# Sandwich layer on one core: three tiles turned by DMA out of SBUF in place of TensorE, Hadamard product a unit later, new order

## Chip, core and metric

The kernel runs on one core of a Trainium2 chip, in one launch. The metric is the device time in microseconds, as the median of the runs. The profile is one execution, with times from the span's start.

## The reference

The input is x of 8 batches x 1024 tokens x 512 features, in float32. Cut to what matters:

```python
def attn(x):                          # 16 heads of 32, causal, score decay of -distance
    Q, K, V = heads(x @ Wq.T + bq), heads(x @ Wk.T + bk), heads(x @ Wv.T + bv)
    s = Q @ K.T / sqrt(32); s = where(future, -inf, s - distance)
    return merge(softmax(s) @ V) @ Wo.T + bo
def ffn(x):                           # H: 512 x 512 Hadamard matrix / sqrt(512)
    xh = x @ H
    scale = max(|xh|, row) / 7; xq = clip(round(xh / scale), -8, 7) * scale
    return xq @ ternary(weight).T
x = x + layernorm(attn(layernorm(x)))
x = x + layernorm(ffn(layernorm(x)))
```

## The kernel before

The 8192 tokens are cut into 32 units of 256 (two tiles t of 128), four units to a batch (PER = 4). A software pipeline runs over steps s. In step s the kernel works on unit n = s+1 (q, k, v products, norms, scores), unit s (keys, exponentials, weighting: the attention proper), unit k = s-1 (output product, first residual, the folded token) and unit k-1 (quantized levels, ternary product, output), while unit m = s+2 is loaded and normalised. Each engine runs its own hand-written list of calls in program order, and semaphores tie the lists together. The order of those lists sets everything, since an engine that waits holds up all that stands behind it. The SP queue is such a list too: it issues all loads and SBUF copies.

Products that must be near float32 are made from float16 pairs (high part, low part) as three matmuls: `split_product`, whose matmuls are all line 1030. `qk(n, g)` for g = 0 to 3 makes a group of q and of k, `values(n, t)` v, `out_product(k, t)` the attention output. The matmul needs the token tile with features on partitions, so the tile has to be turned:

- the normalised token tile: `front_tile` (L1059) turns the float32 tile `xin` on TensorE into a PSUM bank; ACT (`front_high`, L475) and DVE (`front_low`, L743) take the high and low part out of it into `xT`. `qk` and `values` read `xT`.
- the folded token tile (sum and difference of the two halves of x1, `fold`, L832/833): `turn_x2` (L1178), `x2_high` (L534), `x2_low` (L845); `transform` (L1188) then multiplies by the 256 x 256 Hadamard block.
- the level tile q (bfloat16): `find_scale` (DVE) and `round_levels`, `level` (ACT, L540, L546) make it from the Hadamard product; `turn_q` (L1196), `keep_q` (L551); `second` (L1206) multiplies by the ternary weights, and `scale_out`, `z_stats`, `z_columns`, `norm_z`, `finish_out` end the unit.

`keys(s, g, half)` (L1134) makes transposed scores for `exps` (L510, L514), POOL's `clear_future` (L386) clears the future, `weigh(s, g)` (L1154, L1159) multiplies by v. `scores(n, i)` (L1102 to L1114) makes the row maxima for `maxima` (DVE, L767) and needs the stacked q and k parts. Those are made by `restack(n)` on SP (L318): 12 DMAs from `stage` to `stacks`, issued when the last `qk_low_part(n, 3)` (DVE, L753) is done. `max_rows` (L334), `mix_values` (L326 to L328) and the loads of `xres` (L344) and `xin` (L279) are the rest of SP's list.

All products but keys and weighting share four PSUM banks. `ORDER` lists the 24 uses of a step; use i takes bank i % 4, and `claim` makes TensorE wait until the use before it in that bank is emptied.

Of the kernel before, what the change touches and what calls it, by code (L numbers as in the profile page):

```python
# [5 lines left out]
P = 128  # L6
# [27 lines left out]
TP = 2  # L34
# [4 lines left out]
ORDER = (("qk", 0), ("q", 0), ("max", 0), ("qk", 1), ("q", 1), ("qk", 2), ("f", 0), ("qk", 3),  # L39
         ("x", 0), ("f", 1), ("x", 1), ("y", 0), ("y", 1), ("v", 0), ("s", 0), ("norms", 0),  # L40
         ("s", 1), ("v", 1), ("turn", 0), ("turn", 1), ("s", 2), ("s", 3), ("h", 0), ("h", 1))
AHEAD = {"x": 2, "qk": 1, "v": 1, "norms": 1, "s": 1, "max": 0, "y": -1, "turn": -1, "h": -1, "q": -2, "f": -2}

# [22 lines left out]
def fast_path(nc, x, wqT, wkT, wvT, woT, bq, bk, bv, bo, wff, had16, identity, window, ident16,  # L66
# [3 lines left out]
    with ExitStack() as ctx:  # L70
# [20 lines left out]
        xT = [(sb(f"xTh{i}", [P, KC, W2], F16), sb(f"xTl{i}", [P, KC, W2], F16)) for i in range(2)]  # L91
# [9 lines left out]
        ident = sb("ident", [P, P], F32)  # L101
# [9 lines left out]
        xres = sb("xres", [P, TP, D], F32)  # L111
# [3 lines left out]
        x2T = (sb("x2Th", [P, KC, W2], F16), sb("x2Tl", [P, KC, W2], F16))  # L115

        q16 = sb("q16", [P, TP, D], BF16)
        qT = x2T[1][:].bitcast(BF16)
# [17 lines left out]
        y_veps, y_rstd, y_off = col(12), col(14), col(16)  # L136
# [33 lines left out]
        front_turned = sem("front_turned")  # L170
        xTh_made = sem("xTh_made")
        xTl_made = sem("xTl_made")
# [33 lines left out]
        xres_in = sem("xres_in")  # L206
# [8 lines left out]
        x2_turned = sem("x2_turned")  # L215
# [6 lines left out]
        q_turned = sem("q_turned")  # L222
        qT_made = sem("qT_made")
# [51 lines left out]
        def _(sp):  # L275
            def load_front(m):

                until(sp, front_turned, TP * (m - 1))
                sp.dma_start(xin[m % 2][:], rows_of(x, m)).then_inc(xin_in[m % 2], 16)  # L279
# [11 lines left out]
            load_front(0)  # L291
            sp.dma_start(ident[:], identity).then_inc(ident_in, 16)
            load_weights(0, wqT)
            load_weights(1, wkT)
            load_bias(bias[:, 0, :], bq)
            load_bias(bias[:, 1, :], bk)
            load_weights(2, wvT)
            load_weights(3, woT)
            load_bias(bias[:, 2, :], bv)
            load_bias(guard[:, 12:16], bo)  # L300
            sp.dma_start(ffstage, wff.rearrange("(c p) n -> p c n", p=P)).then_inc(ff_in, 16)
            load_front(1)
            sp.dma_start(sel[:], headsel).then_inc(consts_in, 16)
            sp.dma_start(window_sb[:], window).then_inc(consts_in, 16)
            sp.dma_start(identh[:], ident16).then_inc(consts_in, 16)
            sp.dma_start(had[:], had16.rearrange("(c p) n -> p c n", p=P)).then_inc(consts_in, 16)
            sp.wait_ge(w_low, 2)
            load_rows(0)
# [29 lines left out]
            for s in range(-1, STEPS + 1):  # L338
                if has(s):
                    max_rows(s)  # L340
                if has(s - 1):

                    until(sp, x1_made, TP * (s - 1))
                    sp.dma_start(xres[:], rows_of(x, s - 1)).then_inc(xres_in, 16)  # L344
                if has(s + 3) and s + 3 >= 2:
                    load_front(s + 3)
                if has(s + 1):
                    restack(s + 1)
                    mix_values(s + 1)
                if s == -1:  # L350
                    sp.wait_ge(w_low, 4)
                    sp.wait_ge(bv_product, 1)
                    load_rows(1)
                    sp.wait_ge(ff_step, FF_STEPS)
                    load_rows(2)

        @block.gpsimd
        def _(pool):
# [54 lines left out]
            for s in range(-1, STEPS + 2):  # L413
                n, m, k = s + 1, s + 2, s - 1
                if has(m):
                    front_root(m)
                if has(k):
                    heads_low(k, 3)
                if has(n):
                    square_of(n, 0)  # L420
                    square_of(n, 1)
# [3 lines left out]
                if has(k - 1):  # L425
                    z_root(k - 1)
                if has(k):
                    y_root(k)
                if has(s):
                    clear_future(s, 2)  # L430
                    heads_low(s, 0)
                    clear_future(s, 3)
                if has(k - 1):
                    finish_out(k - 1)
                if has(s):
                    heads_low(s, 1)
                    heads_low(s, 2)
# [7 lines left out]
        def _(act):  # L445
# [27 lines left out]
            def front_high(m, t):  # L473
                act.wait_ge(front_turned, TP * m + t + 1)
                nc.scalar.activation(xT[m % 2][0][:, :, t * P:(t + 1) * P],  # L475
                                     bank("x", t)[:].rearrange("p (c n) -> p c n", c=KC), ACT.Copy,
                                     scale=SX).then_inc(xTh_made, 1)
# [53 lines left out]
            def x2_high(k, t):  # L531
                act.wait_ge(x2_turned, TP * k + t + 1)
                until(act, h_product, TP * k + t - 1)
                nc.scalar.activation(x2T[0][:, :, t * P:(t + 1) * P],  # L534
                                     bank("turn", t)[:].rearrange("p (c n) -> p c n", c=KC), ACT.Copy,
                                     scale=SX).then_inc(x2h_made, 1)

            def round_levels(k, t):
                act.wait_ge(qinv_made, TP * k + t + 1)
                nc.scalar.activation(y[:, t, :], bank("h", t)[:], ACT.Identity, bias=round_col[:],  # L540
                                     scale=qinv[:, t:t + 1]).then_inc(rounded, 1)

            def level(k, t):
                act.wait_ge(rounded, TP * k + t + 1)
                until(act, q_turned, TP * (k - 1) + t + 1)
                nc.scalar.activation(q16[:, t, :], y[:, t, :], ACT.Identity, bias=unround_col[:]).then_inc(q_made, 1)  # L546

            def keep_q(k, t):
                act.wait_ge(q_turned, TP * k + t + 1)
                until(act, f_product, TP * k + t - 1)  # L550
                nc.scalar.activation(qT[:, :, t * P:(t + 1) * P],  # L551
                                     bank("q", t)[:, 0:D // 2].bitcast(BF16).rearrange("p (c n) -> p c n", c=KC),
                                     ACT.Copy).then_inc(qT_made, 1)
# [8 lines left out]
            nc.scalar.activation(identb[:], ident[:], ACT.Copy).then_inc(identb_made, 1)  # L562
            front_norm(0, 0)
            front_norm(0, 1)
            weights_high(0)
            front_high(0, 0)
            front_high(0, 1)
            weights_high(1)
            for s in range(-1, STEPS + 2):
# [5 lines left out]
                if has(k - 1):  # L575
                    level(k - 1, 1)
                if s == -1:
                    weights_high(2)
                if has(k - 1):
                    keep_q(k - 1, 0)  # L580
                if has(n):
                    qk_high_part(n, 1)
                if has(m):
                    front_norm(m, 0)
                if has(n):
                    qk_high_part(n, 2)
                if has(m):
                    front_norm(m, 1)
                if has(k - 1):
                    keep_q(k - 1, 1)  # L590
# [1290 lines left out]
```

## Time and profile before

| | us |
|---|---|
| median of 3 runs | 1300.65 (1299.8 to 1302.07) |
| time of the profiled execution | 1295.19 |
| its span | 1293.5 |
| PE busy (matmul) | 1198.1, 93% |
| DVE busy | 1008.5, 78% |
| ACT busy | 714.9, 55% |
| POOL busy | 569.2, 44% |
| SP's DMA queue, share of the 16 DMA engines | 33.3% |

The profiled execution lies 5.46 us below the median of the runs. The page's other parts are the span in slices, the chain of work that ended last (PE 71%, DVE 20%), the groups of instructions and the DMA issues. A busy share is a mean over start, steady part and end; the steady part is read from stretches of the trace.

### The profile page before, as it was taken

Reading aid. Unit: us, or ns where it says so; the run is one execution under the profiler, and the core shown is the slowest. Engines: PE = TensorE matmul, PEld = TensorE weight load, DVE = VectorE, ACT = ScalarE, POOL = GpSimd, SP = SyncE. Lnnn points to the kernel's source line nnn. Section 1 sums busy time; section 2 is a strip of 40 time slices with the busy share of each in tenths; the row PEclk is TensorE's granted clock in tenths of the full one; section 3 lists DMA queues with packets and bytes.
Section 4 is the critical chain, followed back from the end, with each engine's and each line's share of the span. In section 5 each row is a group of like instructions: output and inputs, shape, how many; then the busy total and the mean of one; then the engine's idle time right before and its main releaser. Section 6 shows DMA issues by size and latency. Waiting matters only on the chain.

```text
span 1293.5 us, 45441 instructions
## 1 busy us (share of the span) xinstructions
PE 1198.1 (93%) x19075; PEld 820.7 (63%) x19136; DVE 1008.5 (78%) x2456; ACT 714.9 (55%) x1523; POOL 569.2 (44%) x715
## 2 busy tenths in 40 slices
PE   2779999999999999999999999999999999999852
PEld 2456766666666766666667666667767666676431
DVE  3656887888887888888887888788887888877772
ACT  3444656555665665556556655565565565655531
POOL 0133354454544544544445445544553454444441
PEclk9889999999999999999999999999999999999875
DMA  7333333434344334343443343434433434344110
GB/s 249 90 76 100 101 100 85 115 84 115 85 117 116 89 95 116 84 114 86 116 116 90 95 117 84 115 85 116 116 89 95 116 85 115 84 100 99 53 49 18
DMA packets 69520, 128.50 MB, mean 99 GB/s; under 512 B 14880, under 2 KB 15392, under 8 KB 69216
## 3 DMA queue, kind: packets, MB, share of 16 engines
q1 hardware_dynamic: 64624, 108.50, 33.3%
q0 software_dynamic: 4688, 17.04, 3.5%
q8 instruction: 153, 2.51, 0.8%
q14 instruction: 55, 0.45, 0.1%
HBM read 41.09 MB, written 16.78 MB: 45 GB/s over the span
## 4 chain that ended last, share of the span: by engine, by line
PE 71%; DVE 20%; issue 3%; ACT 3%; SPq 1%; DMA 1%; POOL 0%; POOLq 0%; ACTq 0%; DVEq 0%
PE f_job L1030 41%; PE f_job L1188 5%; PE f_o L1154 5%; PE f_o L1159 4%; PE f_job L1206 4%; PE f_st L1134 3%; DVE f_bst L799 3%; PE f_job L1114 2%; DVE f_y L833 2%; PE f_job L1178 2%; DVE f_x L825 2%; PE f_job L1102 2%; DVE f_y L810 2%; DVE f_xTl L743 1%; PE f_job L1059 1%
## 5 line engine op out<-in xcount | busy, mean ns | idle before, releaser
L386 POOL TENSOR_SCALAR_AFFINE_SELECT f_PT<-f_PT 64x512 f32<-64x512 f32 (+1 forms) x256 | 180.6, 730 | 130.4 <-ACT f_PT L510 93.2
L753 DVE SCALAR_TENSOR_TENSOR f_stage<-f_job,f_bias,f_stage 128x256 f16<-128x256 f32 x256 | 112.0, 479 | 148.3 <-ACT f_stage L488 148.2
L392 POOL TENSOR_TENSOR f_OTl<-f_o,f_OTh 128x256 f16<-128x256 f32 x128 | 89.0, 695 | 290.7 <-ACT f_OTh L528 290.1
L521 ACT ACTIVATE f_inverse<-f_o 128x256 f32<-128x256 f32 x128 | 49.1, 383 | 244.1 <-PE f_o L1159 244.1
L488 ACT ACTIVATE f_stage<-f_job,f_bias 128x256 f16<-128x256 f32 x256 | 106.6, 467 | 109.9 <-PE f_job L1030 109.9
L1030 PE MATMUL f_job<-f_xTh,f_wqh 128*128 128x256 f16 x512 | 140.4, 274 | 7.1 <-DVE f_wkl L652 6.8
L1030 PE MATMUL f_job<-f_xTl,f_wqh 128*128 128x256 f16 x512 | 140.1, 274 | 0.0
L1030 PE MATMUL f_job<-f_xTh,f_wkh 128*128 128x256 f16 x512 | 140.1, 274 | 0.0
L1030 PE MATMUL f_job<-f_xTh,f_wql 128*128 128x256 f16 x512 | 140.1, 274 | 0.0
L1030 PE MATMUL f_job<-f_xTh,f_wkl 128*128 128x256 f16 x512 | 140.1, 274 | 0.0
L1030 PE MATMUL f_job<-f_xTl,f_wkh 128*128 128x256 f16 x512 | 140.0, 273 | 0.0
L401 POOL TENSOR_TENSOR f_square<-f_stage 128x512 bf16<-128x512 f16 x128 | 129.4, 1041 | 15.0 <-ACT f_stage L488 14.9
L510 ACT ACTIVATE f_PT<-f_st 128x512 f32<-128x512 f32 x192 | 108.2, 592 | 30.3 <-PE f_st L1134 30.2
L1030 PE MATMUL f_job<-f_wvh,f_xTh 128*128 128x512 f16 x256 | 98.7, 386 | 0.6 <-DVE f_wvl L652 0.6
L1030 PE MATMUL f_job<-f_wvh,f_xTl 128*128 128x512 f16 x256 | 97.6, 381 | 0.0
L1030 PE MATMUL f_job<-f_wvl,f_xTh 128*128 128x512 f16 x256 | 97.5, 381 | 0.0
L1030 PE MATMUL f_job<-f_woh,f_OTh 128*128 128x512 f16 x256 | 97.5, 381 | 0.0
L1030 PE MATMUL f_job<-f_woh,f_OTl 128*128 128x512 f16 x256 | 97.0, 379 | 0.0
L1030 PE MATMUL f_job<-f_wol,f_OTh 128*128 128x512 f16 x256 | 97.0, 379 | 0.0
L767 DVE TENSOR_REDUCE f_rmax<-f_job 128x8 f32<-128x448 f32 x128 | 76.2, 616 | 20.0 <-PE f_job L1114 19.9
L1134 PE MATMUL f_st<-f_stacks 128*64 128x128 f16 (+1 forms) x2432 | 86.7, 216 | 1.8 <-ACT f_PT L510 1.7
L1134 PEld LDWEIGHTS f_st<-f_stacks 128*64 128x64 f16 x2432 | 67.7, 112 | 30.4 <-issue 24.7
(159 smaller groups left out, 3102.8 us busy)
## 6 DMA issues: line engine op xcount, KB each, us to landing
f_stacks<-f_stage SPq DMA_DIRECT2D x384, 128.0 KB, 2.4
f_xin<-x SPq DMA_DIRECT2D x32, 512.0 KB, 4.7
f_xres<-x SPq DMA_DIRECT2D x32, 512.0 KB, 4.0
out<-f_z POOLq DMA_DIRECT2D x32, 512.0 KB, 4.3
f_Vmix<-f_V SPq DMA_DIRECT2D x32, 256.0 KB, 3.3
f_Vmix<-f_V SPq DMA_DIRECT2D x64, 128.0 KB, 3.4
f_stacks<-rows_const SPq DMA_DIRECT2D x3, 512.0 KB, 5.0
f_stacks<-wqT SPq DMA_DIRECT2D x1, 1024.0 KB, 8.1
```

Of the source, the lines that this page charges most:

```text
L386: nc.gpsimd.affine_select(out=d, in_=d, compare_op=ALU.is_ge, fill=0.0, base=odd * SUB, pattern=[[0, 4], [0, TP], [1, SUB]], channel_multi ...
L392: nc.gpsimd.tensor_tensor(OT[s % 2][1][:, g, :], o32[:, g % 2, :], OT[s % 2][0][:, g, :], ALU.subtract).then_inc(OTl_made, 1)
L401: nc.gpsimd.tensor_tensor(square[:, 2 * m + pair, :], h, h, ALU.mult).then_inc(squared, 1)
L488: nc.scalar.activation(stage[:, 2 * m, g, :], bank("qk", g)[:, m * W2:(m + 1) * W2], ACT.Identity, bias=bias[:, m, g:g + 1]).then_inc(qk_h ...
L510: nc.scalar.activation(dst, src, ACT.Exp, scale=1.0 / SS).then_inc(expd, 1)
L753: nc.vector.scalar_tensor_tensor(stage[:, 2 * m + 1, g, :], bank("qk", g)[:, m * W2:(m + 1) * W2], bias[:, m, g:g + 1], stage[:, 2 * m, g, ...
L767: nc.vector.tensor_reduce(rmax[:, n % 2, SLOTS * i:SLOTS * i + SLOTS], bank("s", i)[:, 0:SLOTS * BW].rearrange("q (i k) -> q i k", k=BW), ...
L1030: mm = pe.matmul(dst, lhs[a](c), rhs[b](c), start=(n == 0), stop=(n == 3 * KC - 1))
L1134: mm = pe.matmul(ps_st[half][upper * SUB:(upper + 1) * SUB, i * W2 + q * SUB:i * W2 + (q + w) * SUB], Ks[js % 3][:, h, c * SUB:(c + 1) * SUB],
L1154: pe.matmul(dst[rows, c * SUB:(c + 1) * SUB], v[:, g * P + r * HD:g * P + (r + 1) * HD], weights[keys, r, c * SUB:(c + 1) * SUB], start=Tr ...
L1159: mm = pe.matmul(dst[r * HD:(r + 1) * HD, W2 + lo:W2 + hi], ones[keys], weights[keys, r, lo:hi], start=True, stop=True)
L1188: mm = pe.matmul(dst, x2T[h][:, 2 * half + c, t * P:(t + 1) * P], had[:, c, :], start=(h == 0 and c == 0), stop=(h == 1 and c == 1))
```

## The change

- The three turns leave TensorE. ACT and DVE now split the untransposed tile in SBUF: `front_high(m)` and `front_low(m)` one instruction each over 128 x 1024 (`xh`, `xl`), `x2_high`, `x2_low` over 128 x 512 (`x2h`, `x2l`). SP turns them with DMA transposes: 2 a unit of 128 x 1024 (`turn_x`), 4 of 128 x 512 (`turn_x2`), 2 of 128 x 512 (`turn_q`). `front_tile`, TensorE's `turn_x2` and `turn_q`, and `keep_q` are gone.
- `transform` and what follows it (`find_scale`, `round_levels`, `level`) run one step later, on unit k-1; `second` stays in that step, further back.
- `round_levels` writes back into the PSUM bank in place of `y`; the residual input is loaded straight into `x1` and `xres` is gone; `xT`, `x2T`, `qT` are laid out tile by tile.
- `ORDER` has 18 uses, and the lists of PE, ACT, DVE, POOL and SP are in a new order.

```diff
 def turn_x(m):                                         # SP, all new
+    sp.wait_ge(xl_made, m + 1)
+    until(sp, v_product, TP * (m - 1))
+    for half, src in enumerate((xh, xl)):
+        sp.dma_start(xT[m % 2][half][:]..., src[:]..., transpose=True).then_inc(x_turned, 16)
+def turn_x2(k, t):
+    sp.wait_ge(x2l_made, TP * k + t + 1)
+    until(sp, h_product, TP * (k - 1) + t + 1)
+    for half, src in enumerate((x2h, x2l)):
+        sp.dma_start(x2T[half][:, t], src[:, t, :], transpose=True).then_inc(x2_turned[t], 16)
+def turn_q(k, t):
+    sp.wait_ge(q_made, TP * k + t + 1)
+    until(sp, f_product, TP * (k - 1) + t + 1)
+    sp.dma_start(qT[:, t], q16[:, t, :], transpose=True).then_inc(q_turned[t], 16)
```

The lists of a step, before and after (each call under its condition on the unit):

```text
SP before:  max_rows(s) xres(k) load_front(m+1) restack(n) mix_values(n)
SP after:   max_rows(s) load_res(k) turn_q(k-1,0) turn_q(k-1,1) restack(n) turn_x(m)
            load_front(m+1) mix_values(n) turn_x2(k,0) turn_x2(k,1)
PE before:  qk0 turn_q0 turn_max qk1 turn_q1 qk2 second0 qk3 keys(0,0) keys(0,1) front_tile0 second1
            front_tile1 keys(1,0) keys(1,1) out0 out1 weigh0 keys(2,0) keys(2,1) values0 weigh1
            scores0 norms scores1 keys(3,0) keys(3,1) values1 turn_x2_0 turn_x2_1 scores2 weigh2
            scores3 transform0 weigh3 transform1
PE after:   qk0 turn_max qk1 qk2 transform(k-1,0) qk3 transform(k-1,1) keys(0,0) keys(0,1) out0
            keys(1,0) keys(1,1) out1 weigh0 keys(2,0) weigh1 second0 second1 values0 keys(2,1)
            keys(3,0) scores0 keys(3,1) norms scores1 weigh2 values1 scores2 scores3 weigh3
ACT after:  keep_max high0 high1 high2 heads_high3 round_levels0 level0 front_norm0 high3 exps(0,0)
            exps(0,1) front_norm1 front_high exps(1,0) round_levels1 exps(1,1) level1 invert0
            exps(2,0) invert1 heads_high0 exps(2,1) exps(3,0) keep_v0 x2_high0 exps(3,1) keep_v1
            x2_high1 heads_high1 invert2 norm_z invert3 heads_high2
DVE after:  front_stats low0 normalise3 find_scale0 low1 front_offset low2 find_scale1 low3 y_out0
            front_low y_out1 y_stats normalise0 scale_out0 residual scale_out1 fold0 z_stats x2_low0
            maxima0 keep_norms normalise1 maxima1 fold1 maxima2 z_columns maxima3 split_max x2_low1
            normalise2 x_stats
```

## Rows read from the trace of the kernel before

**Rows 1.** Stretch table of the steady part: length, busy per engine, clock, DMA.

```profile
core 0: us, PE busy (x) PEld busy (x) DVE busy (x) ACT busy (x) POOL busy (x), PEclk, DMA share, GB/s
180.00:1180.00 1000.00, 988.42 (x16070) 683.37 (x16123) 825.23 (x2021) 590.06 (x1271) 477.78 (x593) 1.00 0.39 102
```

**Rows 2.** Timeline of SP: start, length, line, count.

```profile
80.33 7.75 SPq L318 DMA_DIRECT2D f_stacks<-f_stage  x12
...
186.68 3.90 SPq L318 DMA_DIRECT2D f_stacks<-f_stage  x6
...
595.66 4.68 SPq L318 DMA_DIRECT2D f_stacks<-f_stage  x6
...
1186.40 9.01 SPq L318 DMA_DIRECT2D f_stacks<-f_stage  x12
```

**Rows 3.** Groups of instructions: the turns on TensorE.

```profile
L1178 PE MATMUL f_job<-f_ident,f_y 128*128 128x128 f32 x256 | 38.8, 288 | 17.4 <-DVE f_y L833 9.2 <-DVE f_nmax L759 6.1 <-DVE f_rmax L767 1.0
...
L1059 PEld LDWEIGHTS f_job<-f_ident,f_xin 128*128 128x128 f32 x256 | 29.9, 143 | 23.8 <-issue 16.3
...
L1178 PEld LDWEIGHTS f_job<-f_ident,f_y 128*128 128x128 f32 x256 | 29.8, 145 | 31.2 <-issue 10.2 <-DVE f_nmax L759 9.2 <-DVE f_rmax L767 8.4
...
L1196 PEld LDWEIGHTS f_job<-f_identb,f_q 128*128 128x128 bf16 x256 | 19.6, 99 | 10.9 <-issue 9.6
```

**Rows 4.** Timeline of PE, first half of a step (qk0 starts at 617.72).

```profile
617.72 0.27 PE L1030 MATMUL f_job<-f_xTh,f_wqh 128*128 128x256 f16 x1
...
626.52 0.81 PE L1206 MATMUL f_job<-f_ternT,f_x2Tl 128*128 128x512 bf16 x3
627.17 0.27 PE L1030 MATMUL f_job<-f_xTh,f_wqh 128*128 128x256 f16 x1
...
630.48 0.66 PE L1059 MATMUL f_job<-f_ident,f_xin 128*128 128x128 f32 x4
631.19 0.38 PE L1206 MATMUL f_job<-f_ternT,f_x2Tl 128*128 128x512 bf16 x1
...
632.37 0.67 PE L1134 MATMUL f_st<-f_stacks 128*64 128x128 f16 x20
632.97 0.39 PE L1030 MATMUL f_job<-f_woh,f_OTh 128*128 128x512 f16 x1
...
638.25 0.32 PE L1154 MATMUL f_o<-f_PT,f_Vmix 128*32 128x64 f32 x8
```

**Rows 5.** Timeline of PE, end of the step before (scores0, transform0, weigh3).

```profile
607.35 0.37 PE L1102 MATMUL f_job<-f_window,f_identb 128*32 128x448 bf16 x4
...
614.84 0.39 PE L1188 MATMUL f_job<-f_had,f_x2Th 128*128 128x256 f16 x2
...
615.82 0.32 PE L1154 MATMUL f_o<-f_PT,f_Vmix 128*32 128x64 f32 x8
```

**Rows 6.** Groups of instructions: ACT's exponentials and levels.

```profile
L510 ACT ACTIVATE f_PT<-f_st 128x512 f32<-128x512 f32 x192 | 108.2, 592 | 30.3 <-PE f_st L1134 30.2
...
L540 ACT ACTIVATE f_y<-f_job,f_round_col,f_small 128x512 f32<-128x512 f32 x64 | 49.2, 769 | 13.9 <-DVE f_small L862 13.8
L546 ACT ACTIVATE f_q<-f_y,f_unround_col 128x512 bf16<-128x512 f32 x64 | 45.6, 712 | 0.1
```

**Rows 7.** DMA issues: size and median us from issue to landing.

```profile
f_stacks<-f_stage SPq DMA_DIRECT2D x384, 128.0 KB, 2.4
```

**Rows 8.** Timeline of SP at the start: bias columns, written in 4-byte pieces.

```profile
3.40 1.86 SPq L286 DMA_DIRECT2D f_bias<-bk  x1
...
12.39 0.74 SPq L286 DMA_DIRECT2D f_guard<-bo  x1
```

**Rows 9.** Stretch table around two waits of TensorE early in the run.

```profile
75.44:77.34 1.90, 0.00 (x1) 0.00 (x1) 1.90 (x2) 1.57 (x6) 1.90 (x4) 1.00 0.00 0
77.70:81.00 3.30, 3.30 (x58) 1.92 (x59) 3.27 (x11) 1.28 (x4) 0.82 (x2) 0.50 0.03 5
84.93:87.80 2.87, 0.00 (x0) 0.00 (x0) 1.28 (x3) 0.80 (x2) 1.72 (x3) 1.00 0.92 205
87.80:90.00 2.20, 0.00 (x0) 0.03 (x1) 0.00 (x0) 0.00 (x0) 0.00 (x0) 0.50 0.67 145
90.00:94.60 4.60, 4.60 (x104) 2.73 (x105) 1.85 (x3) 1.48 (x5) 0.30 (x1) 0.50 0.01 4
```

More of the change, by code:

```diff
@@ L205, in fast_path @@
         OTl_made = sem("OTl_made")
-        xres_in = sem("xres_in")
+        xres_in = [sem(f"xres_in{i}") for i in range(2)]
         back_step = sem("back_step")
@@ L214, in fast_path @@
         folded = sem("folded")
-        x2_turned = sem("x2_turned")
+        x2_turned = [sem(f"x2_turned{t}") for t in range(TP)]
         x2h_made = sem("x2h_made")
@@ L339, in _ @@
+            sp.dma_start(identh[:], ident16).then_inc(consts_in, 16)
+            sp.dma_start(had[:], had16.rearrange("(c p) n -> p c n", p=P)).then_inc(consts_in, 16)
+            sp.wait_ge(w_low, 2)
+            load_rows(0)
+            for s in range(-1, STEPS + 2):
+                n, m, k = s + 1, s + 2, s - 1
                 if has(s):
                     max_rows(s)
-                if has(s - 1):
-                    until(sp, x1_made, TP * (s - 1))
-                    sp.dma_start(xres[:], rows_of(x, s - 1)).then_inc(xres_in, 16)
@@ L345, in _ @@
[L345 to L349, printed above, removed]
-                if s == -1:
[L351 to L355, printed above, removed]
+                if has(k):
+                    load_res(k)
+                if has(k - 1):
+                    turn_q(k - 1, 0)
+                    turn_q(k - 1, 1)
@@ L357, in _ @@
+                if has(n):
+                    restack(n)
+                if has(m):
+                    turn_x(m)
+                if has(m + 1):
+                    load_front(m + 1)
+                if has(n):
+                    mix_values(n)
+                if has(k):
+                    turn_x2(k, 0)
+                if s == -1:
+                    load_rest()
+                if has(k):
+                    turn_x2(k, 1)
         @block.gpsimd
@@ L414, in _ @@
                 n, m, k = s + 1, s + 2, s - 1
+                if has(n):
+                    square_of(n, 0)
                 if has(m):
@@ L1172, in out_product @@
                               [lambda c, h=h: W["o"][h][:, c, :] for h in range(2)]).then_inc(y_product, 1)
-            def turn_x2(k, t):
-                claim("turn", t, k)
-                pe.wait_ge(folded, 2 * (TP * k + t) + 2)
-                for c in range(KC):
-                    mm = pe.transpose(bank("turn", t)[:, c * P:(c + 1) * P], y[:, t, c * P:(c + 1) * P], ident[:])
-                mm.then_inc(x2_turned, 1)
             def transform(k, t):
                 claim("h", t, k)
-                pe.wait_ge(x2l_made, TP * k + t + 1)
+                pe.wait_ge(x2_turned[t], 32 * (k + 1))
                 for half in range(2):
@@ L1187, in transform @@
                         for c in range(2):
[L1188 removed]
+                            mm = pe.matmul(dst, x2T[h][:, t, 2 * half + c, :], had[:, c, :],
                                            start=(h == 0 and c == 0), stop=(h == 1 and c == 1))
                 mm.then_inc(h_product, 1)
[L1192 to L1198 removed]
             def second(k, t):
@@ L1215, in _ @@
                     qk(n, 0)
-                if has(k - 1):
-                    turn_q(k - 1, 0)
                 if has(s):
@@ L1221, in _ @@
                     qk(n, 1)
-                if has(k - 1):
-                    turn_q(k - 1, 1)
-                if has(n):
                     qk(n, 2)
                 if has(k - 1):
-                    second(k - 1, 0)
+                    transform(k - 1, 0)
                 if has(n):
                     qk(n, 3)
+                if has(k - 1):
+                    transform(k - 1, 1)
                 if has(s):
@@ L1247, in _ @@
                     keys(s, 2, 0)
-                    keys(s, 2, 1)
+                    weigh(s, 1)
+                if has(k - 1):
+                    second(k - 1, 0)
+                    second(k - 1, 1)
                 if has(n):
```

385 lines of the change are left out of this document (169 added, 216 removed).

## The prediction

> **What bounds the kernel now.** I read the page first: TensorE (PE) is busy 93% of the span, and that number mixes the slow start and end with the middle. So the second view is a stretch table of the middle: in 1000 us PE is busy 988, at full clock, while DVE has 825 and ACT 590 [rows 1]. The middle is bound by PE's own list of work, back to back. The third view is SP's timeline: from the restack that starts at 186.68 to the one that starts at 1186.40 there are 27 steps, 37.03 us each [rows 2]. PE work taken away is worth its full length only as long as nothing else in the step comes late; so for each wait of PE's list I ask how much room it has now and what room it has in the new order. The timeline of one step gives that: from PE's rows I take start-to-start distances, since matmuls overlap and their lengths overstate them.
>
> **What leaves PE.** The turns cost what their weight loads take: 29.9, 29.8 and 19.6 us over the run [rows 3], 0.93, 0.93 and 0.61 us a step, 2.47 together, 79 us in all. PE also waits 17.4 us in front of the folded token's turn, for DVE [rows 3]; that wait goes too. So 96 us at most if nothing comes late. A step would be 37.03 - 2.47 - 17.4 / 32 = 34.0 us.
>
> **What moves to ACT, DVE, POOL: nothing on the path.** ACT loses two evictions of the level tile and gets two instructions on SBUF tiles of the same total size as before; DVE's low parts have the same sizes; both have room (17% and 41% idle in [rows 1], of a step that PE sets). POOL's list is permuted. If DVE's order went wrong, its cover would be these 6 us a step. I cost them at zero. The residual's load moves from `xres` to `x1` and stays early in SP's list, far ahead of its reader.
>
> **What moves to SP, and what stands behind it.** This is the step that decides. SP's list is in order. Before, `restack(n)` is issued as soon as the stage is full: at 595.66, 11.7 us before PE starts scores0 at 607.35 [rows 2, 5]. What it needs is known from step 1, where PE stood waiting for it: restack starts at 80.33 and PE resumes at 90.00 [rows 2, 9], 9.67 us for 12 issues of about 0.6 us (7.75 together) and the last landing (2.4 us, [rows 7]). So there are 2.0 us of room now. In the new list `turn_q(k-1,0)` and `turn_q(k-1,1)` stand in front of restack, and the second waits for `level(k-1,1)`, which ACT does only after exps(1,0), round_levels1 and exps(1,1). When is that, from the start of qk0?
>
> - PE reaches keys(1,0) before at 632.37 - 617.72 = 14.65 [rows 4]. Out go the level turns (0.61), two `second` (627.17 - 626.52 = 0.65 each) and the token turns (631.19 - 630.48 = 0.71 each); in come two transforms (615.82 - 614.84 = 0.98 each, [rows 5]) and one output product (half of 638.25 - 632.97, 2.64). 14.65 - 0.61 - 1.30 - 1.42 + 1.96 + 2.64 = 15.92; half a keys group (0.30) makes it 16.2.
> - ACT then does exps, round_levels, exps, level: 0.59 + 0.77 + 0.59 + 0.71 = 2.66 [rows 6]. The level tile is there at 18.9.
> - SP issues its turn: D, unknown. Then restack to scores0: 9.67. Scores0 can start at 28.6 + D.
> - PE's own work would bring it there at 34.0 less what follows. What follows: before 617.72 - 607.35 = 10.37 [rows 4, 5], less the folded turn 0.93, the transforms 1.96 and a half of keys 0.30, thus 7.18. So PE is there at 26.8 and waits 1.8 + D.
> - The step is 28.6 + D + 7.18 = 35.75 + D.
>
> Queued behind that waiting `turn_q` are restack, the next `turn_x`, the input load, `mix_values` and both `turn_x2`; only restack is late at once. `second` itself is not: the level tile lands at 18.9 + D + 1.8 (2.4 us from issue to landing in [rows 7], less the issue's own 0.6), and the 1.8 + D us in front of scores0 swallow its delay.
>
> **D.** No transposing DMA is in this trace. From below: 0.6, what SP takes for any plain DMA of 128 KB (7.75 / 12, [rows 2]). From above: a turned 128 x 512 tile is four 128 x 128 blocks; four plain issues are 2.4. The nearest rows by kind are the bias columns, also scattered over partitions in small pieces: 0.74 and 1.86 [rows 8], mean 1.3. I take 1.3 and keep 0.6 and 2.4 as ends. A step is then 37.05 us, as long as the 37.03 of now. The Trainium skill is of two minds here. Its page "Advanced Engine Details and Errata" (X-Bar Transpose) calls such DMAs as fast as regular ones; that would be the lower end. Its page "DMA: Bandwidth & Descriptors" (the table on the fast descriptor path) gives the generation before 262,144 cycles of the sequencer for 8,192 tiles, 32 a tile, and elsewhere speaks of 256-byte tiles (SDMA does more than copy); at 1.2 GHz, 512 tiles of a 128 KB transfer would be an estimated 13.7 us. No run here shows either yet.
>
> **The clock.** A new wait of 1.8 + 1.3 = 3.1 us in every step also touches PE's clock. In the trace a wait of 5.07 us (84.93 to 90.00) is followed by 1.2 GHz from 87.8 on, for 4.6 us of work after PE resumes, and one of 1.90 us by at least 3.3 us at 1.2 GHz [rows 9]. In those stretches work takes up to twice as long, so one fall costs at most 4.6 / 2 = 2.3 us. Scores with their small matmuls lose less, and not each wait need bring a fall: I take 0.8 us a step, with 0 and 2.3 as ends. This agrees with the Trainium skill ("TensorE: Matmul & The Clock Gate", Part 1), by which an idle PE drops to the half clock and sustained work brings it back; a wait longer than the work it replaces can so cost more than itself.
>
> **Start and end.** At the start `turn_x(0)` is hidden behind the weight loads that the first product waits for. In the last unit nothing covers the turns: the folded tile goes through 2 D + 1.8 = 4.4 us of DMA in place of a turn of 0.93, the level tile through D + 1.8 = 3.1 in place of 0.61. 6 us more.
>
> **Sum.** (37.05 + 0.8 - 37.03) x 31 = 25, and 6: 1295.2 + 31 = 1326 for the profiled execution, which lies 5.5 below the median: 1332.
>
> **Rivals.**
> - *The gain survives because the turn is cheap and the clock holds.* D = 0.6 and no fall: a step of 36.35, -0.68 x 31 = -21, end +5, 1279, as a median 1284. For it: SP's plain issues are 0.6 whatever their size. Against: a wait of 2.4 us in each step, and the clock fell after 1.90. It decides below D = 1.3 with a steady clock, below 0.5 with my 0.8. Chance 0.20.
> - *Restack is not late.* If ACT had level1 done before 15.9 us, the 96 us come whole: 1295 - 96 + 6 = 1205, as a median 1211. Against: PE's list alone puts keys(1,0) at 16.2. Chance 0.10.
> - *SP, or the DMA engines behind it, become the bound.* A step holds 19 plain DMAs (11.4 us) and turns of ten times 128 KB: 11.4 + 10 D fills 37 us at D = 2.6. Earlier, at D = 2.4, `turn_x` (two of 4.8 us behind restack) lands at 18.9 + 2.4 + 7.75 + 9.6 + 2.4 = 41.05, where the next qk0 waits: +4.0 x 31 = 124, end +8, 1427, as a median 1433; each further us of D then costs 10 us a step, 310 us. Against: the DMA engines are busy 0.39 now [rows 1], and 1.25 MB a step more are a third of what they move. The long figure of the skill's table would be this case. Chance 0.20.
> - *It cancels*: D near 1.1 with a rare fall of the clock. Chance 0.05.
>
> **How the numbers follow.** The forecast, slower by a late restack, holds 0.45, with its own range 1302 to 1400. About 0.2% is what a measurement of this kernel can tell from no change. Faster: 0.20 + 0.09 = 0.29; same 0.06; slower 0.65. The range goes down to 1250, which leaves out most of the 1211 case (0.08), and up to 1440, which leaves out the longer part of the SP case (0.12).
>
> **What would show it.** SP's timeline: the length of a transpose issue of 128 KB (D), and restack starting about 19 + D after qk0 and 9.7 ahead of scores0, in place of 11.7. The waits: PE at L1102 for the DMA to `stacks`, some 3 us in each step, and none at L1178's place. The granted clock of the middle: below 1.00 in some slices. PE busy falls by some 80 us while the span does not. Wrong would make it: a D outside 0.6 to 2.4, a PE wait for `xT` at qk0 or for `x2T` at transform ahead of the one at scores0, or ACT so late with level1 that the wait grows without D.

## The result and the profile after

The changed kernel takes 1395.62 us as the median of 4 runs (1392.61 to 1398.35), beside 1301.36 us (1299.8 to 1303.37) for the kernel before on the same chip: a ratio of 1.0723, 95% interval 1.0693 to 1.0753. The forecast was 1332, +2.4%. The sign is right and the size is not: the kernel is slower by 7.2%. 1395.62 lies within 1250 to 1440.

The stretch table of the changed kernel, for the 1000 us that [rows 1] showed of before:

```profile
core 0: us, PE busy (x) PEld busy (x) DVE busy (x) ACT busy (x) POOL busy (x), PEclk, DMA share, GB/s
180.00:1180.00 1000.00, 900.21 (x14105) 583.20 (x14132) 703.05 (x1827) 513.74 (x1085) 425.24 (x544) 0.93 0.59 126
```

PE was busy 988 of 1000 us at full clock and is busy 900 at a mean of 0.93, with 14105 matmuls in place of 16070. No other engine has become full: DVE fell from 825 to 703, ACT from 590 to 514. So PE waits, and part of its work runs at the lower clock. The chain that ended last, as the page gives it, names SP's restack and its landing, where before it was 71% PE and 20% DVE:

```profile
PE 59%; SPq 20%; DMA 8%; issue 4%; ACT 4%; DVE 3%; POOL 1%; POOLq 0%; DVEq 0%; ACTq 0%
PE f_job L1046 37%; SPq L322 16%; DMA f_stacks<-f_stage 6%; PE f_job L1185 4%; PE f_o L1158 3%; PE f_st L1138 3%; PE f_o L1163 3%; PE f_job L1106 3%; PE f_job L1118 3%; SPq L307 3%; ACT f_job L574 2%; ACT f_x2h L579 1%; PE f_job L1094 1%; DMA f_x2Tl<-f_x2l 1%; DMA f_xin<-x 1%
```

In the list of waits scores0 (now L1106) waits 31 times for restack (115.2 us in total, 7.1 the longest). Now one step, which answers to [rows 2, 4, 5]. First SP's timeline (start, length):

```profile
630.27 7.88 SPq L307 DMA_TRANSPOSE f_qT<-f_x2h  x2
638.25 9.05 SPq L322 DMA_DIRECT2D f_stacks<-f_stage  x12
```

L307 is `turn_q`, L322 restack. In the changed kernel the level tile q lies in the memory of `x2h`, so the views call it f_x2h. ACT's timeline of the same step, the level that the second `turn_q` waits for:

```profile
636.24 0.70 ACT L579 ACTIVATE f_x2h<-f_job,f_unround_col 128x512 bf16<-128x512 f32 x1
```

PE's timeline, from one qk0 through scores0 to the next qk0:

```profile
618.24 0.28 PE L1046 MATMUL f_job<-f_xTh,f_wqh 128*128 128x256 f16 x1
...
649.31 0.56 PE L1106 MATMUL f_job<-f_window,f_identb 128*32 128x448 bf16 x4 [4.40 <-DMA f_stacks<-f_stage]
...
659.05 0.28 PE L1046 MATMUL f_job<-f_xTh,f_wqh 128*128 128x256 f16 x1
```

The level is done at 636.94 and SP begins restack at 638.25: 1.31 us for the turn between them, the D of the prediction. Restack starts 20.0 us after qk0 and PE stands at scores0 from 26.7 on (forecast 20.2 and 26.8). But the wait is 4.40 us, scores0 to the next qk0 takes 9.74 in place of 7.18, and the step is 40.81. Between 300 and 1150 us the 21 waits of scores0 for restack add up to 79.0 us, 3.8 each. Means over the middle are taken here and below over the 26 steps from the fifth restack to the last but one: the step is 40.47 us (before 37.06), restack starts 20.1 us and scores0 30.7 us after qk0, and from scores0 to the next qk0 it is 9.8 us.

What the clock does around that wait, in the stretch table (from the start of the wait to the next qk0):

```profile
644.90:648.00 3.10, 0.01 (x1) 0.00 (x0) 2.39 (x6) 1.90 (x4) 1.28 (x2) 1.00 0.61 134
648.00:649.30 1.30, 0.00 (x0) 0.02 (x1) 0.00 (x0) 0.00 (x0) 0.00 (x0) 0.52 0.97 196
649.30:654.90 5.60, 5.59 (x137) 3.25 (x138) 3.71 (x8) 0.60 (x1) 2.56 (x4) 0.50 0.68 167
654.90:659.05 4.15, 4.15 (x131) 2.29 (x129) 1.29 (x4) 1.92 (x5) 0.45 (x1) 1.00 0.06 14
```

PE idles for 4.4 us. The granted clock falls during the idle time, stays at 0.50 (1.2 GHz) for the first 5.6 us of work after it, and is back at 1.00 from 654.9 on. The step pays for its wait twice. One such fall in each step also gives the middle's mean: full clock less (1.3 + 5.6) x 0.5 / 40.8 is 0.92, as it is over 300:1150. In the trace the clock falls in each of the 26 steps of the middle. It also hides the gain from PE's busy time: that fell by 11.6 us (1198.1 to 1186.5) and not by the forecast 80, since work at the lower clock counts for longer.

The 102.1 us between the two spans (1395.6 and 1293.5) divide like this. The first restack starts at 45.74 (before 40.13), 5.6 us; the last at 1285.19 (before 1186.40), so the 31 steps between cost 98.8 - 5.6 = 93.2 us, 3.0 each (3.4 in the middle, less in the first steps); what is left, 102.1 - 98.8 = 3.3, is the end.

### The profile page after: what moved, and what is told of

Its sections match the earlier page's. It is cut to its first block, busy times and chain, and to the rows that moved or that the text cites. A ratio compares the mean times of both kernels' runs of the same rounds, so it can differ in the third digit from the quotient of the medians.

```text
span 1395.6 us, 44026 instructions
## 1 busy us (share of the span) xinstructions
PE 1186.5 (85%) x18337; PEld 763.0 (55%) x18368; DVE 943.7 (68%) x2424; ACT 680.6 (49%) x1427; POOL 554.9 (40%) x715
## 2 busy tenths in 40 slices
DMA packets 241548, 170.39 MB, mean 122 GB/s; under 512 B 186912, under 2 KB 187424, under 8 KB 241248
## 4 chain that ended last, share of the span: by engine, by line
PE 59%; SPq 20%; DMA 8%; issue 4%; ACT 4%; DVE 3%; POOL 1%; POOLq 0%; DVEq 0%; ACTq 0%
PE f_job L1046 37%; SPq L322 16%; DMA f_stacks<-f_stage 6%; PE f_job L1185 4%; PE f_o L1158 3%; PE f_st L1138 3%; PE f_o L1163 3%; PE f_job L1106 3%; PE f_job L1118 3%; SPq L307 3%; ACT f_job L574 2%; ACT f_x2h L579 1%; PE f_job L1094 1%; DMA f_x2Tl<-f_x2l 1%; DMA f_xin<-x 1%
## 5 line engine op out<-in xcount | busy, mean ns | idle before, releaser
L421 POOL TENSOR_SCALAR_AFFINE_SELECT f_PT<-f_PT 64x512 f32<-64x512 f32 (+1 forms) x256 | 164.5, 663 | 485.0 <-ACT f_PT L546 362.9
L782 DVE TENSOR_REDUCE f_rmax<-f_job 128x8 f32<-128x448 f32 x128 | 79.3, 621 | 161.9 <-PE f_job L1118 161.9
L1106 PE MATMUL f_job<-f_window,f_identb 128*32 128x448 bf16 x512 | 59.1, 444 | 115.2 <-DMA f_stacks<-f_stage 115.2
L532 ACT ACTIVATE f_V<-f_job 128x512 f32<-128x512 f32 x64 | 38.4, 599 | 184.7 <-PE f_job L1046 184.6
L1046 PE MATMUL f_job<-f_wvh,f_xTh 128*128 128x512 f16 x256 | 106.6, 416 | 5.6 <-DVE f_stage L768 5.6
L825 DVE SCALAR_TENSOR_TENSOR f_y<-f_job,f_bo_bc 128x512 f32<-128x512 f32 x64 | 44.3, 692 | 92.5 <-PE f_job L1046 92.5
L1046 PE MATMUL f_job<-f_wvh,f_xTl 128*128 128x512 f16 x256 | 104.8, 409 | 0.0
L1046 PE MATMUL f_job<-f_wvl,f_xTh 128*128 128x512 f16 x256 | 102.2, 399 | 0.0
L1138 PEld LDWEIGHTS f_st<-f_stacks 128*64 128x64 f16 x2432 | 71.7, 115 | 49.8 <-issue 45.4
L1163 PE MATMUL f_o<-f_PT,f_ones 128*32 128x256 f32 (+2 forms) x1280 | 98.2, 384 | 0.3 <-issue 0.3
```

Of the source, the lines that this page charges most:

```text
L421: nc.gpsimd.affine_select(out=d, in_=d, compare_op=ALU.is_ge, fill=0.0, base=odd * SUB, pattern=[[0, 4], [0, TP], [1, SUB]], channel_multi ...
L782: nc.vector.tensor_reduce(rmax[:, n % 2, SLOTS * i:SLOTS * i + SLOTS], bank("s", i)[:, 0:SLOTS * BW].rearrange("q (i k) -> q i k", k=BW), ...
L1046: mm = pe.matmul(dst, lhs[a](c), rhs[b](c), start=(n == 0), stop=(n == 3 * KC - 1))
L1106: pe.matmul(dst[rows, 0:SLOTS * BW], identb[:, rows], window_sb[:, at0:at0 + SLOTS * BW], start=True, stop=False)
L1138: mm = pe.matmul(ps_st[half][upper * SUB:(upper + 1) * SUB, i * W2 + q * SUB:i * W2 + (q + w) * SUB], Ks[js % 3][:, h, c * SUB:(c + 1) * SUB],
L1163: mm = pe.matmul(dst[r * HD:(r + 1) * HD, W2 + lo:W2 + hi], ones[keys], weights[keys, r, lo:hi], start=True, stop=True)
```

## The experiments

All ratios are against the kernel before, timed on the same chip. The kernel before took 1300.8 us beside experiments 1 to 4, 1295.0 beside 5 to 7, 1293.4 beside 8 and 1291.2 beside 9, so between these groups the ratios are to be compared and not the times. In the diffs `-` is the changed kernel, unless another base is named.

**1. ACT makes the second level early.** The levels' second half stands right behind `exps(s,0,*)`:

```diff
 ACT: exps(s,0,0) exps(s,0,1)
+     round_levels(k-1,1) level(k-1,1) exps(s,1,0)
      front_norm(m,1)
-     front_high(m) exps(s,1,0) round_levels(k-1,1) exps(s,1,1) level(k-1,1)
+     exps(s,1,1) front_high(m)
```

> Only ACT's order: round_levels1 and level1 directly behind exps(0,1), the second front_norm and front_high behind exps(1,0). The changed kernel has a step of 40.5 us, restack starting 20.0 us after qk0, a wait of 4.4 us at scores0 and PE at half clock behind it. Theory 1 (restack is late, and the wait drops PE's clock): level1 is ready 2.9 us earlier, the wait shrinks to 1.5 us, the clock mostly holds and 2.5 us more a step come back: a step near 35.5 and some 1240 us. Rival 1 (the clock fall costs no more than the 0.8 us of the prediction): only 2.9 to 3.7 us a step, 1280 to 1305 us. Rival 2 (SP or the DMA engines are the bound): no change, 1395.

Measured: 1315.53 us, ratio 1.0116 (1.0091 to 1.0141), 80 us less than the changed kernel. The forecast of 1240 is missed by 75 us, and the time lies 10 us above the first rival's range (1280 to 1305), but the wait did what was worked out for it. Restack starts 17.1 us after qk0, the wait for it falls from 115.2 to 40.5 us in all, the middle's clock rises from 0.92 to 0.98, and the step is 37.67. So `turn_q` in front of restack, held by ACT's second level, carries most of the loss. Part of what is left shows in DVE's timeline, and in POOL's of the same time:

```profile
642.24 3.46 DVE L760 SCALAR_TENSOR_TENSOR f_xl<-f_xin,f_xh 128x1024 f16<-128x1024 f32 x1 [2.43 <-ACT f_xh L513]
```

```profile
641.33 1.28 POOL L421 TENSOR_SCALAR_AFFINE_SELECT f_PT<-f_PT 64x512 f32<-64x512 f32 x2 [2.45 <-ACT f_PT L546]
642.58 2.03 POOL L436 TENSOR_TENSOR f_square<-f_stage 128x512 bf16<-128x512 f16 x2
```

DVE's low part of the token tile waits for ACT's high part, which now stands behind two more exponentials, and then takes 3.46 us (mean 3317 ns; in the changed kernel 1217). It ends at 645.70, 1.1 us after POOL's squares end at 644.61, and alone it takes 1.22: it seems to have done its work only then. The clock also still falls in 14 of the 26 steps. Experiments 5, 7 and 8 come back to this.

**2. PE kept busy in the wait.** Sixteen matmuls of 128 x 512 whose result nobody reads stand in front of scores0's wait:

```diff
 def scores(n, i):                       # i == 0, ahead of the wait for restack
+    for _ in range(16):
+        pe.matmul(bank("s", 0)[:], W["q"][0][:, 0, 0:P], W["q"][0][:, 0, :], start=True, stop=True)
```

> The changed kernel with 16 matmuls of 128x512 more in each step (3.45 us at full clock), written into scores0's bank ahead of its wait for the restack, where they are overwritten. Theory 1 (the fall of the clock behind the wait costs 2.5 us a step): PE does 110 us more work and the kernel is still faster, by up to 2.5 x 31 = 78, near 1320 us, with the granted clock of the middle at 1.00. Rival 1 (the long tail behind the wait comes from DVE, ACT or from contention with DMAs and not from the clock): 1395 or a little slower.

Measured: 1351.78 us, ratio 1.0397 (1.0364 to 1.0431). The kernel does more work and is 44 us faster than the changed one. The stretch table of the middle, first the changed kernel, then this one:

```profile
300.00:1150.00 850.00, 766.01 (x11988) 494.95 (x12008) 594.90 (x1547) 435.30 (x921) 360.23 (x460) 0.92 0.59 125
```

```profile
300.00:1150.00 850.00, 837.64 (x12942) 531.87 (x12940) 626.02 (x1628) 456.65 (x964) 378.81 (x484) 1.00 0.61 132
```

The clock stays at 1.00. Scores0 starts no earlier (30.9 us after qk0, in the changed kernel 30.7), but the tail behind it takes 7.8 us, in the changed kernel 9.8. So a fall of the clock costs 2.0 us a step, and the tail at full clock is 0.6 longer than the 7.18 of the prediction. Of the 2.0 us, 1.6 lie between scores0 and `values(n,1)`, in keys, norms, scores and weighting (4.47 us against 2.85 with the filling), and 0.4 in `values(n,1)`: the clock is back before most of its matmuls start. The step of the middle shrinks by 1.8 us to 38.70, over all 31 steps it is 1.4 each; theory 1's 78 us was the most that 2.5 could give.

**3. The same DMAs without turning.** Every transpose is issued as a plain DMA of the same bytes, so that nothing is turned and the output isn't the reference's:

```diff
-    sp.dma_start(qT[:, t], q16[:, t, :], transpose=True)
+    sp.dma_start(qT[:, t].rearrange("p c n -> p (c n)"), q16[:, t, :])     # turn_x, turn_x2 alike
```

> The changed kernel with all eight turns as plain DMAs of the same bytes and the same waits, so that nothing is turned (the products work on tiles that are not transposed). It takes away what a transposing DMA costs over a plain one: issue 1.3 to 0.6 us, and the load on the DMA engines (0.55 of their time after, 0.39 before). Theory 1: the wait at scores0 shrinks by 0.7 (issue) and by the 1.3 that restack's issues now take longer, to 2.4 us; the clock falls less often or not at all: 1260 to 1335 us. Rival 2 (it is the time of the transposes on the DMA engines that counts): more than that, under 1240. Rival 3 (the kind of DMA does not matter, only the order): 1370 or more.

Measured: 1352.8 us, ratio 1.0405 (1.0367 to 1.0443). D is 0.6 us here, the mean wait at scores0 3.1 and the step 39.26. The time lies above theory 1's range (1335) and below rival 3's (1370). Even a turn as cheap as a plain DMA would have left the kernel slower than before: 43 of the 94 us between the two kernels hang on the turns being transposes, and 51 on the rest, their place in the lists and the new order, which no run takes apart. The first rival (D = 0.6, the gain survives) fails on its second condition: the clock of the middle is 0.95.

**4. Restack ahead of the level turns.**

```diff
 SP: max_rows(s) load_res(k)
+    restack(n)
     turn_q(k-1,0) turn_q(k-1,1)
-    restack(n)
```

> Only SP's order: restack(n) ahead of both turn_q. Theory 1: restack starts 14.9 us after qk0 and scores0 no longer waits, but the turns of the level tile now stand behind 12 issues and land at 25 and 26.4 us, where PE wants them at 22: the wait moves to second0, about 4 us, and the clock falls as before: 1375 to 1400 us. Rival (the wait for restack alone is the loss): 1395 - 4.4 x 31 = 1259 us.

Measured: 1415.01 us, ratio 1.0884 (1.0849 to 1.0918), the slowest of all and 15 us over theory 1's range. The wait has only moved: the waits name scores0 for 8.0 us in all, and the second product for 131.6, as in this row of PE's timeline:

```profile
651.48 1.02 PE L1195 MATMUL f_job<-f_ternT,f_qT 128*128 128x512 bf16 x4 [4.19 <-DMA f_qT<-f_x2h]
```

With 12 restack issues ahead of them the two turns of the level are issued 11.5 and 6.2 us later than in the changed kernel (23.6 and 25.0 us after qk0), and `second` stands before scores0 on PE. Neither order of the two on SP serves both; the level itself has to come earlier.

**5. The whole token chain early on ACT.** From experiment 1, with `front_high` ahead of the exponentials of group 1, so that DVE's low part meets POOL idle:

```diff
 ACT: exps(s,0,0) exps(s,0,1)
+     round_levels(k-1,1) level(k-1,1)
      front_norm(m,1) front_high(m)
      exps(s,1,0)
-     round_levels(k-1,1)
      exps(s,1,1)
-     level(k-1,1)
```

> The changed kernel with ACT's order: exps(0,1), round_levels1, level1, front_norm1, front_high, exps(1,0), exps(1,1). The earlier run with level1 early had front_high after exps(1,1), and DVE then stood 2.4 us before front_low, which took 3.46 us beside POOL's work in place of 1.22. Theory 1 (what was left of that run's loss, a step of 37.7 against 34.0 of PE work, is DVE held up by front_low): front_low lies between y_out0 and y_out1 again, DVE gets some 4 us back, only the wait of 1.2 us at scores0 stays: a step near 35.5, 1240 us. Rival (DVE's own list, or the DMA load, bounds the step at 37.7): 1305 to 1320.

Measured: 1263.66 us, ratio 0.9763 (0.9735 to 0.979), faster than both kernels, though 24 us over the forecast of 1240. The stretch table of the middle, first of the kernel before, then of this one:

```profile
300.00:1150.00 850.00, 841.06 (x13684) 581.58 (x13729) 703.85 (x1725) 502.49 (x1083) 407.21 (x506) 1.00 0.39 102
300.00:1150.00 850.00, 818.13 (x13595) 542.68 (x13617) 675.91 (x1760) 491.49 (x1045) 409.82 (x521) 1.00 0.67 142
```

and its group of the low part:

```profile
L758 DVE SCALAR_TENSOR_TENSOR f_xl<-f_xin,f_xh 128x1024 f16<-128x1024 f32 x32 | 39.2, 1225 | 30.5 <-ACT f_xh L513 30.4
```

The low part is back at 1225 ns, the clock at 1.00, the step at 35.74. PE's work is 818.13 / 850 x 35.74 = 34.4 us a step, before 841.06 / 850 x 37.06 = 36.7: 2.3 less, and the prediction had 2.47 for the turns. That part of the change does what was worked out. The clock, which fell in 14 of 26 steps of experiment 1, falls in one here, so not all of the 1.9 us a step between the two runs is DVE's low part. What keeps the step over PE's own 34.4 is still restack: SP's timeline of one step,

```profile
647.07 5.03 SPq L307 DMA_TRANSPOSE f_qT<-f_x2h  x2
652.20 8.55 SPq L322 DMA_DIRECT2D f_stacks<-f_stage  x12
```

has it start at 652.20, 17.2 us after a qk0 at 635.04. Scores0 waits for it 39.1 us in all; between 300 and 1150 us it is 24 waits of 25.8 us together, 1.1 each.

**6. More PE work ahead of scores0.** From experiment 5, with `values(n,1)` ahead of scores0 to fill that wait, and what follows moved along on ACT and DVE:

```diff
 PE:  ... keys(3,0)
+     values(n,1)
      scores0 keys(3,1) norms scores1 weigh2
-     values(n,1)
      scores2 scores3 weigh3
 DVE:
-     maxima0 keep_norms
      normalise1
-     maxima1
      fold1
+     maxima0 keep_norms maxima1
 ACT: heads_high0
-     exps(2,1) exps(3,0)
      keep_v0
+     exps(2,1) exps(3,0)
      x2_high0
-     exps(3,1)
      keep_v1
+     exps(3,1)
      x2_high1
```

> The same, and values1 (2.65 us) ahead of scores0 on PE, with keep_v0 ahead of exps(2,1) and keep_v1 ahead of exps(3,1) on ACT, and normalise1 and fold1 ahead of maxima0 on DVE. Scores0 is then due 29.4 us after qk0 and restack lands at 28.1: no wait on the DMA is left. Theory 1: a step of 34.0 to 34.6, 1200 to 1225 us, granted clock 1.00. Rival (the maxima, now in the last 4.5 us of a step, hold up the next qk0 and turn_max): no better than the run beside it, 1235 or more.

Measured: 1308.72 us, ratio 1.0098 (1.0067 to 1.0128): a miss, 45 us slower than its base. The wait for restack is gone (3.3 us in all), but the tail that `values(n,1)` had filled is now a row of short matmuls that wait for others: the step is 37.55, and the clock falls in 16 of the 26 steps (0.97 in the middle). For several of PE's waits at `scores` and `weigh` in the tail the trace names no releaser, so which of the moved calls is to blame stays open.

**7. The token tile alone.** The kernel before, unchanged but for its token tile, which is split in SBUF and turned by DMA behind restack; the folded and the level tile stay on PE:

```diff
 # base: the kernel before
-PE:  front_tile(m,0) front_tile(m,1)
-ACT: front_high(m,0) front_high(m,1)     DVE: front_low(m,0) front_low(m,1)
+ACT: front_high(m)                       DVE: qk_low_part(n,3) front_low(m)
+SP:  restack(n) turn_x(m)
```

> The kernel before with one part of the change alone: the token tile is split in SBUF and turned by two DMA transposes, issued by SP behind restack; folded and level tiles are turned on TensorE as before and all orders stay. Theory 1 (a turn on PE costs its issue time, a turn by DMA costs nothing where nothing is queued behind it): PE loses 29.9 us of weight loads and restack starts as early as before: 1265 to 1280 us. Rival 1 (DMA transposes slow other work by their load on SBUF or on the DMA engines): 1300 or more. Rival 2 (restack's landing becomes late beside the turns): a wait at scores0 and the clock falls, 1320 or more.

Measured: 1334.61 us, ratio 1.0318 (1.0283 to 1.0353): a miss. The profiled execution (1325.07) is the fastest of the four. Its span is 29.9 us over that of before (1323.4 and 1293.5): 7.4 come from the start, where `turn_x(0)` stands ahead of the bias loads as in the changed kernel (see experiment 9; the first restack at 47.56, before 40.13), and 22.8 from the 31 steps. No DMA is waited for in the middle, and the clock is 1.00. DVE is late. Its timeline, and POOL's:

```profile
648.26 1.88 DVE L752 SCALAR_TENSOR_TENSOR f_xl<-f_xin,f_xh 128x1024 f16<-128x1024 f32 x1 [1.04 <-ACT f_xh L489]
```

```profile
645.03 4.04 POOL L414 TENSOR_TENSOR f_square<-f_stage 128x512 bf16<-128x512 f16 x4
649.02 1.66 POOL L399 TENSOR_SCALAR_AFFINE_SELECT f_PT<-f_PT 64x512 f32<-64x512 f32 x1
```

The low part starts at 648.26 while POOL's squares run until 649.07, and ends at 650.14, again 1.1 us after them. POOL pays too (its second row is from a narrower stretch): the mask that starts at 649.02 beside it takes 1.66 us, the three behind it 1.89 together. From there DVE runs nearly without idle time up to the maxima, behind which the folded token's turn on PE waits: at L1170 weight loads stand 31.7 us and matmuls 20.0 us waiting for them, before 8.4 and 1.0 [rows 3].

**8. The same with the split in DVE's idle time.** From experiment 7:

```diff
 ACT: front_norm(m,1)
+     front_high(m)
      keep_q(k-1,1) ... exps(s,0,1)
-     front_high(m)
 DVE:
+     front_low(m)
      qk_low_part(n,3)
-     front_low(m)
```

> The kernel before with the token tile alone turned by DMA, as in the run before it, and one difference: ACT makes the high part right after front_norm(m,1), and DVE the low part ahead of qk_low_part(n,3), where it stood idle for 2.0 us of the step, and no longer behind it. Theory A (that run lost its time because the split stood in the full part of DVE's list: 1.0 us of waiting for ACT and 1.9 us of a low part slowed by POOL's squares and masks beside it, which made DVE late for the folded token's turn): the low part falls back to about 1.2 to 1.5 us, DVE's wait for ACT's high part nearly goes, PE's wait at the folded token's turn shrinks to what it is in the kernel before (17 us in the run), and the time is 1262 to 1285, faster than before by 1 to 3%. Theory B (the DMA turn or the copies behind it disturb the kernel, wherever the split stands): 1325 to 1340 as before. Between the two (1290 to 1315) the place carries only part of it.

Measured: 1306.0 us, ratio 1.0101 (1.0074 to 1.0129). It lies between the two theories, takes back about two thirds of experiment 7's loss and is no gain, so the place carries most, not all. The group of the low part:

```profile
L751 DVE SCALAR_TENSOR_TENSOR f_xl<-f_xin,f_xh 128x1024 f16<-128x1024 f32 x32 | 39.2, 1225 | 12.4 <-ACT f_xh L489 12.4
```

It is 1225 ns again, with 12.4 us of waiting in place of 33.6. The span is 10.8 us over that of before (1304.3 and 1293.5): 6.6 come from the start (the first restack at 46.77, before 40.13), as in experiment 7, and 5.9 from the 31 steps between the first restack and the last (37.17 each, before 36.98); the end is 1.8 shorter. The 0.93 us that PE no longer needs for the token's turns doesn't shorten the step, since in this order PE waits for DVE at the folded token's turn: its matmuls stand 29.6 us waiting there, before 17.4 [rows 3]. The turn is paid in waiting instead.

**9. The first turn behind the loads.** From experiment 5. At the start SP's timeline of the changed kernel shows a gap between 2.80 and 20.40:

```profile
2.29 0.51 SPq L280 DMA_DIRECT2D f_stacks<-wkT  x1
20.40 1.37 SPq L294 DMA_TRANSPOSE f_xTh<-f_xh  x1
...
23.18 0.58 SPq L284 DMA_DIRECT2D f_bias<-bq  x1
```

`turn_x(0)` waits for DVE's low part, and the loads of the bias columns and all others stand behind it; before they were issued from 2.82 on.

```diff
 SP:  load_front(0) ident wqT wkT
-     turn_x(0)
      bq bk wvT woT bv bo wff load_front(1) headsel window ident16 had16
+     turn_x(0)
```

> The kernel with the token chain early in ACT's list (1263.66 us, ratio 0.9763) and one difference: turn_x(0) stands behind SP's last constant load, no longer ahead of the bias columns. In the changed kernel SP stands at it until 20.4 us, and the fifteen loads behind it are issued 18 us later than before; ACT then waits 11.5 us for the scaled bias, and the first restack starts at 45.7 in place of 40.1. Theory A (the loads behind the waiting turn cost the start its 5.6 us): the first restack starts at 40 to 42, ACT's wait for the bias is gone, and the time falls by 3 to 6 us, to 1257 to 1261, ratio about 0.972. Theory B (the start is set by the turned tile or by the weights, and the bias was hidden): the first restack stays at 45 and the time at 1262 to 1266.

Measured: 1268.36 us, ratio 0.9826 (0.9796 to 0.9857), no gain over experiment 5 (0.9763). Neither theory's range holds; each is half right. ACT's wait for the bias is gone, but now PE waits for the turned tile until 28.3 us; the first restack starts at 43.93, 1.4 earlier and not 4 to 5. The steps of the middle are 35.98 in place of 35.74, which the edit doesn't explain (the clock falls in three of the 26 steps in place of one); over the run that is more than what the start gave.

## Why the prediction was wrong in size

The direction and the mechanism stand: PE's list got shorter, restack got late behind `turn_q`, and the wait at scores0 and the clock behind it took more than the turns gave. The step that failed is the price of the clock, 0.8 us a step, which measured 2.0. Point by point:

- *What leaves PE* (2.47 us a step): right, 2.3 by experiment 5. The "96 us if nothing comes late", a step of 34.0, was not in reach: PE's work alone is 34.4 there. The sum spread PE's 17.4 us of waiting for DVE over the 32 steps, but 9.2 of them are two single waits (<-DVE f_y L833 in [rows 3]) outside 300:1150, and PE's idle time of all kinds in the middle of before is (850 - 841.06) / 850 x 37.06 = 0.39 us a step.
- *The level tile at 18.9, restack at 20.2, PE at the wait at 26.8*: right. Measured 18.7 (636.94 - 618.24), 20.0 and 26.7.
- *D = 1.3*: right, 1.31 by ACT's and SP's rows. That the value hit is luck: it was the mean of two bias loads of 0.74 and 1.86 us, and no row tied these to a transpose. The lower end, a transpose as cheap as a plain DMA, is not what the traces show. The Trainium skill ("Advanced Engine Details and Errata", X-Bar Transpose) calls the two equally fast; this trace shows 1.3 against 0.6 us to issue and 2.5 to 4.0 against 2.4 us to land, so it doesn't agree. The 13.7 us that the prediction gave as an estimate beside it is ten times the measured 1.3.
- *Restack to scores0 in 9.67*: too short. It came from one restack in step 1, when nothing else was moving [rows 2, 9]. In the step above it is 649.31 - 638.25 = 11.06, over the middle 10.6; scores0 starts 30.7 after qk0, where 28.6 + 1.3 = 29.9 was forecast: 0.8 us a step. A row of before had already said so: its last restack took 9.01 us for the 12 issues [rows 2]; the mean of its middle is 8.2, of the changed kernel's 8.5. The transposes are not the reason: with plain DMAs (experiment 3) restack to scores0 takes 10.7.
- *Tail of 7.18*: 0.6 short (7.8 at full clock in experiment 2).
- *The clock, 0.8 us a step*: **this is the step that failed most**, a term that was mis-sized. A fall costs 9.8 - 7.8 = 2.0 us, and the clock falls in every step of the middle. The prediction named 2.3 as the most a fall could cost and then took a third of it, on the argument that scores with their small matmuls lose less and that not each wait brings a fall. Both halves failed: all 26 steps have the fall, and 1.6 of the 2.0 us are lost in just these small matmuls ahead of `values(n,1)` (experiment 2).
- Sum: 0.8 + 0.6 + (2.0 - 0.8) = 2.6 us a step over the 37.85 of the forecast, thus 40.45; measured 40.47 in the middle. Over the 31 steps the loss was 93.2 in place of 25.
- *Start and end, 6*: 8.9. The start was costed at nothing, "hidden behind the weight loads". The transposes were, but not what SP had queued behind the first: 5.6 us. The end took 3.3 in place of 6.

The rivals. That the gain survives with a cheap turn fell with experiment 3. That restack isn't late fell too, though experiment 5 brings the level in time: there the level's turn is issued 15.8 us after qk0, within the 15.9 of the rival, but the time is 1263.66 and not 1211. Restack still ends a wait of 1.1 us a step, since it takes 10.8 us to reach PE and not 9.67, and PE's work is 34.4 and not 34.0. That SP or the DMA engines become the bound is not what happened: a transpose of 256 KB is issued in 1.30 to 1.33 us (medians), hardly longer than most of 128 KB (1.22), so a step has 8 turns of some 1.3 and not 10 D, and the DMA engines' share is 0.59.

What experiments 1, 5, 7 and 8 show beside that: the prediction costed the split in SBUF at zero, as "same sizes" with idle time as cover. The change's own order happened to place it well (1217 ns), and so the term didn't count there; in two other orders the instruction was 0.55 and 2.1 us longer in the mean (1778 and 3317 ns).

## What to carry to other kernels

Work taken from the bounding engine is worth its length only up to the next wait in the step; before moving a job into an in-order queue, write down what stands behind its wait there, and take the times of the jobs behind it from the busy middle of the run, not from a quiet step at its start. A new wait of TensorE in every step should be costed with the fall of the clock in full (here 3.8 us of waiting and 2.0 more of slow work), and filling it with work that nobody needs is a quick test of that. When a wait comes from an order, move the producer up (here ACT's level and high part: the ratios are 1.0723 for the changed kernel and 0.9763 for experiment 5, which do the same work) rather than the consumer's DMA.

## What the runs showed of the hardware

- A DMA transpose from SBUF to SBUF took 1.3 us of SP's queue where a plain DMA took 0.6. The medians between 300 and 1150 us of the changed kernel are 1.22 us for the level tile, 1.26 and 1.72 for the two parts of the folded tile (the longest 2.8) and 1.30 and 1.33 for the token tile, which has twice the bytes. Medians from issue to landing are 2.5 us for the level tile, 3.3 for the token tile, 3.5 and 4.0 for the folded tile. With all turns as transposes the DMA engines' share of the middle is 0.59, as plain DMAs 0.47, before 0.39. The same 170.4 MB went in 241548 packets with transposes and in 106380 without (experiment 3); 186912 and 18976 of them were under 512 bytes.
- With waits of TensorE of 3.8 us in the mean the granted clock fell in every step of the middle; in the step shown it stood at 0.50 for 1.3 us of the wait and for 5.6 us of work after it. With waits of 1.1 us in the mean (experiment 5) it fell in one step of 26.
- A DVE instruction with both inputs in SBUF (128 x 1024, 1.22 us) took 1.88 and 3.46 us when it started while POOL was squaring or masking in SBUF. It ended 1.1 us after the last square in both rows, and in the first (experiment 7) the mask that POOL started beside it took 1.66 us, the next three 1.89 together. This agrees with the Trainium skill ("SBUF — State Buffer", the section on SBUF's two separate sides), by which such a DVE instruction and a GpSimd one that reads SBUF hold a shared port in turn. In the second row DVE got its turn only behind the rest of a mask and two squares that followed each other; no run shows why not between them. The low part that read its first input from PSUM took 685 ns for 128 x 512 and is not that kind.
